# Register loads moved ahead of waits, and one root moved to ScalarE, in a two-layer graph network kernel

## The chip, the cores and the metric

One core of a Trainium2 chip. The metric is the device time of one execution in microseconds; the kernel before has a median of 3344.86 us over 3 runs (3327.63 to 3351.23). Its parts run on five engines with queues of their own: PE (matmul), DVE (vector), ACT (ScalarE), POOL (GpSimd) and SP, tied together by semaphores written out by hand.

## What is computed

A graph of 6250 nodes with 128 channels and 106250 edges, sorted by destination. First an attention layer, then an edge network with a sum over the incoming edges, each followed by a layer norm:

```python
hi, hj = x[src] @ w1, x[tgt] @ w2
logits = (leaky_relu(hi + hj, 0.3) * a).reshape(-1, 8, 16).sum(-1)
attn = exp(logits - segment_max) / segment_sum          # per destination
x = layernorm(x + segment_sum(hi * attn, tgt))
ef = (relu(edge_attr @ We1 + be1) @ We2 + be2) * sigmoid(ts @ Wt + bt)
msg = relu(concat([x[row], ef]) @ Wn1 + bn1) @ Wn2 + bn2
x = layernorm(x + segment_sum(msg, col) + x)
```

A layer norm divides by sqrt(variance + 1e-5).

## The kernel before

The edges are cut into NQ = 208 groups of 512 (QE). Destinations are sorted, so a group touches a window of at most 64 nodes (W) that begins at a base. The bases stand in `baseR`, and the columns of the table of hj that belong to a group in `tabR`, both in SBUF. Everything runs twice over the edges.

**Attention loop** (`run_steps`). A step handles GQ = 3 groups; there are NG = 70 steps, the last with one group. POOL (L707) gathers rows of `hi_rows` by index, 128 rows at a time, 4 gathers a group, into a ring of RG = 4 steps. On PE, `sums` adds to the transposed rows (L1826) the destination's part (L1831), ScalarE and DVE form the leaky value (L895, L1307), `quad_logits` (L1787) the logits. DVE scans for the maxima, makes one-hots of the window (L1389) and the messages (L1336), and `aggregate` on PE sums messages (L1854) and exponentials (L1858) over the window. DVE's `add` (L1310 to L1320) adds these sums at the window's base into `acc`. An `add` waits for `s_agg` (the sums) and `s_acc` (its own last add), then loads the base into a register, then adds. In `sums` PE waits for logits, gathered rows (`s_g`) and one-hots, and then loads the column. Batches of 3 node blocks (MB) are normalised in between. POOL waits for the messages of 3 steps ago before it refills a slot.

**Between the loops** the last steps A, Z and O (3, 3 and 1 groups) are written out, with adds of their own (L1442), then the last node blocks are normalised (L1404 to L1430) and written to `y_rows`. POOL waits for that write before it starts the second loop. In the drains PE runs some matmuls whose results nobody reads (`hold`, L1932, and L2055).

**Edge loop** (`run_edges`). One group a turn, in stages that lag each other: q is loaded and transposed, q-2 goes through the first layer (L2081, L1006), q-4 through the second (L2075) and the sigmoid (L994, L1629), q-6 is multiplied (L2069), added to the gathered row of `y_rows` (L1619) and passed through Relu (L999), q-8 is summed over the window (L2060) and added by DVE at its base (L1613). POOL (L741) gathers 4 times a group, up to 8 groups ahead of L1619. When a node block is complete (LOOPED = 45 of NB = 49 in the loop, one for every fourth group), PE multiplies its sum (L2096), DVE adds it to the row (L1578), takes moments (L1582, L1589), the reciprocal root, and scales (L1597); SP writes it out.

**The end.** After the last group DVE waits, PE multiplies the last 4 blocks (`rest`, L2101), and `finish`, `scale` and `normalise` do the same for all four at once, with tiles of 128x4. The reciprocal root of `inverse_root` is an iteration on DVE: variance + eps (L1167), two integer instructions (L1168, L1169) and three turns of three (L1171 to L1173), each waiting for the one before by semaphore `s_f["nr"]`, 11 counts (NEWTON) for each block.

ScalarE needs a function table in place: Exp in the attention loop, Sigmoid in the edge loop; Copy and Relu run with either.

Of the kernel before, what the change touches and what calls it, by code (L numbers as in the profile page):

```python
# [73 lines left out]
def build(nc, x, src, dst, attr, ew, w1, w2, a, We1, be1, We2, be2, Wt, bt, Wn1, bn1, Wn2, bn2,  # L74
          hi_d, y_d, x1_d, rel_d, scan_d, max_d, sum_d, agg_d, out):
    with ExitStack() as ctx:
# [703 lines left out]
        def _(act):  # L780
# [200 lines left out]
            with act.Else():  # L981
# [5 lines left out]
                def edge(q, r, k, m):  # L987
# [8 lines left out]
                    if z is not None:  # L996
                        act.wait_ge(s_b["zs"], z + 1)
                        need(act, s_b["agg"], z - 1)
                        act.activation(hS[i], zS[i], ACT.Relu).then_inc(s_b["h"], 1)  # L999
                        if not is_int(z) or z + RB < NQ:  # L1000

                            stage_b(z + RB, (r - L_Z) % RB)
                    if h is not None:
                        act.wait_ge(s_b["h1"], h + 1)
                        need(act, s_b["ef"], h - 1)
                        act.activation(r1S[i], h1P[i][:, :], ACT.Relu, bias=cols[:, 1:2]).then_inc(s_b["r1"], 1)  # L1006
                    if r % BQ == 0 and m is not None and (not is_int(m) or m < LOOPED):
                        act.wait_ge(s_b["acc"], (m + (LAG - 2)) * BQ)
                        need(act, s_f["o"], m)
                        act.activation(aF, accH[:, bass.ds(m * P, P)], ACT.Copy).then_inc(s_f["copy"], 1)  # L1010
                run_edges(act, edge)

        @block.vector
        def _(dve):
# [265 lines left out]
            with dve.Else():  # L1282
# [13 lines left out]
                def step(g, s, n, m):  # L1296
# [12 lines left out]
                    def add(j):  # L1309
                        if p is None or j >= quads(p):  # L1310
                            return
                        dve.wait_ge(s_agg, p * GQ + j + 1)
                        need(dve, s_acc, 2 * (p * GQ + j))
                        if is_int(p) and p == 0 and j == 0:
                            dve.wait_ge(s_zero, 18)
                        base = dve.value_load(baseR[0:1, bass.ds(p * GQ + j, 1)], min_val=0, max_val=NODES - 1)  # L1316
                        w_ = acc[:, 0, bass.ds(base, W)]
                        dve.tensor_tensor(w_, AG[j % 2][:, 0:W], w_, ALU.add).then_inc(s_acc, 1)  # L1318
                        w_ = accD[:, bass.ds(base, W)]
                        dve.tensor_tensor(w_, AG[j % 2][0:DC, W:2 * W], w_, ALU.add).then_inc(s_acc, 1)  # L1320
# [253 lines left out]
            with dve.Else():  # L1574
# [26 lines left out]
                def edge(q, r, k, m):  # L1601
# [3 lines left out]
                    if ends and r % BQ == 2:  # L1605
                        dve.wait_ge(s_x2, m + 1)
                        finish(m, 1, oP[:, 0:C], X1[:, bass.ds(m, 1), :].rearrange("p b c -> p (b c)"), xF, yF)
                    if g4 is not None:
                        dve.wait_ge(s_b["agg"], g4 + 1)
                        need(dve, s_b["acc"], g4)  # L1610
                        base = dve.value_load(baseR[0:1, bass.ds(g4, 1)], min_val=0, max_val=NODES - 1)
                        w_ = accH[:, bass.ds(base, W)]
                        dve.tensor_tensor(w_, sums_of(g4), w_, ALU.add).then_inc(s_b["acc"], 1)  # L1613
                    if z is not None:
# [32 lines left out]
                run_edges(dve, edge)  # L1647
                dve.wait_ge(s_x2, NB)
                finish(LOOPED, rest, ps[6][:, 0:rest * C], X1[:, LOOPED:NB, :].rearrange("p b c -> p (b c)"), xr, yr)
                scale(LOOPED, rest)  # L1650
                normalise(LOOPED, rest, xr, yr)


# [3 lines left out]
        def _(pe):  # L1657
# [125 lines left out]
            with pe.Else():  # L1783
# [17 lines left out]
                def step(g, s, n, m):  # L1801
# [7 lines left out]
                    def sums(j, of=None, os_=0, lj=0):  # L1809


                        if j >= nq:
                            logits(of, os_, lj)
                            return
                        lone = of is None or lj >= quads(of)
                        if not lone:
                            pe.wait_ge(s_lk, of * GQ + lj + 1)
                        pe.wait_ge(s_g[s][j], 64 * (n + 1) - 16 * (is_int(f) and f == NG - 1))
                        q = f * GQ + j
                        pe.wait_ge(s_ohT, q + 1)  # L1820
                        need(pe, s_lk, (f - 1) * GQ + j + 1)
                        col = pe.value_load(tabR[0:1, bass.ds(q, 1)], min_val=0, max_val=(2 * NB - 1) * 3 * C)

                        for i in range(4):
                            t = 4 * j + i
# [310 lines left out]
```

## Time and profile before

| what | value |
|---|---|
| median of 3 runs | 3344.86 us (3327.63 to 3351.23) |
| span of the profiled execution | 2205.4 us |
| busy: PE, DVE, ACT, POOL | 1817.9, 1325.7, 658.7, 1607.1 us |
| granted clock of PE, mean | 0.892 of full |
| chain that ended last, by engine | POOL 51%, issue 21%, PE 15%, DVE 5%, DMA 4% |
| gathers of the attention loop (L707) | 831, 804.1 us busy, 968 ns each |
| gathers of the edge loop (L741) | 831, 788.0 us busy, 948 ns each |
| adds in the attention loop's `add` (L1318), in the edge loop (L1613) | 201, 208, each 225 ns |

The span runs from the first to the last instruction of one execution under the profiler. The median of the runs is 1139.5 us longer; what lies in that difference the profile does not show. "issue" is time in which an engine waited for nothing that the profile shows. The chain is followed back from the last instruction to whatever released it, so it tells which engine's work set the end, where busy shares only tell who worked much.

### The profile page before, as it was taken

The numbers are of one execution on the slowest core, as the hardware profiler recorded it, in microseconds if no ns is written. First come the engines' busy times: TensorE is split into PE (matmuls) and PEld (weight loads), VectorE is DVE, ScalarE is ACT, GpSimd is POOL, SyncE is SP. The second block draws the span as 40 slices with busy tenths as digits, with TensorE's granted clock in tenths as the row PEclk, the third lists the DMA queues.
The fourth block names the chain that finished last, engine by engine and source line by source line (L and its number), as shares of the span: only waits on it lengthen the run. The fifth ranks groups of instructions, "written<-read, shape, count | busy, mean of one in ns | idle before, by whom it ended". The sixth has DMA issues, their size and how long they took to land.

```text
span 2205.4 us, 47181 instructions
## 1 busy us (share of the span) xinstructions
PE 1817.9 (82%) x12720; PEld 1413.0 (64%) x12721; DVE 1325.7 (60%) x3725; ACT 658.7 (30%) x1410; POOL 1607.1 (73%) x1701
## 2 busy tenths in 40 slices
PE   6778888888887788888879888888888888788887
PEld 6455666666665566666657667666766676667665
DVE  6454667565665666656645456666566666665665
ACT  6111112111121111111114344444444444444432
POOL 5777777777777777777517777777777777777775
PEclk9897879888799989888869999999999999899898
DMA  8722333333333333333245444444444444444441
GB/s 233 153 82 84 82 85 102 89 95 85 94 96 84 95 88 96 92 87 95 60 135 154 129 135 127 141 127 142 134 134 128 140 127 141 126 142 130 137 126 45
DMA packets 239385, 252.30 MB, mean 114 GB/s; under 512 B 141011, under 2 KB 187720, under 8 KB 239315
## 3 DMA queue, kind: packets, MB, share of 16 engines
q1 hardware_dynamic: 185036, 141.15, 21.5%
q0 software_dynamic: 54000, 110.28, 19.4%
q8 instruction: 30, 0.49, 0.1%
q14 instruction: 31, 0.25, 0.0%
q10 hardware_dynamic: 288, 0.13, 0.0%
HBM read 233.20 MB, written 13.22 MB: 112 GB/s over the span
## 4 chain that ended last, share of the span: by engine, by line
POOL 51%; issue 21%; PE 15%; DVE 5%; DMA 4%; DVEq 1%; POOLq 1%; ACT 1%; SPq 0%; ACTq 0%
POOL T L741 31%; POOL G L707 20%; PE ps L1854 3%; PE ps L1831 2%; DMA G<-hi_rows,idx 2%; PE ps L1826 2%; PE ps L1858 2%; PE ps L1787 1%; PE ps L2069 1%; DVEq L1316 1%; DVE msg L1336 1%; PE ps L2060 1%; DMA T<-y_rows,idx 1%; PE ps L2075 0%; ACT V L895 0%
## 5 line engine op out<-in xcount | busy, mean ns | idle before, releaser
L741 POOL DMA_INDIRECT T<-y_rows,idx x831 | 788.0, 948 | 310.2 <-issue 249.4
L707 POOL DMA_INDIRECT G<-hi_rows,idx x831 | 804.1, 968 | 263.3 <-issue 248.4
L2060 PE MATMUL ps<-G 128*128 128x64 f32 x1664 | 227.3, 283 | 117.5 <-DVE acc L1613 116.9
L999 ACT ACTIVATE G<-G 128x512 f32<-128x512 f32 x208 | 131.0, 630 | 582.4 <-DVE G L1619 582.4
L2060 PEld LDWEIGHTS ps<-G 128*128 128x128 f32 x1664 | 216.0, 203 | 129.4 <-issue 128.9
L1826 PE MATMUL ps<-ident,G 128*128 128x128 f32 x828 | 151.1, 312 | 161.7 <-issue 81.0
L1619 DVE TENSOR_TENSOR G<-ps,T 128x512 f32<-128x512 f32 x208 | 143.6, 690 | 225.9 <-DMA T<-y_rows,idx 217.4
L2069 PE MATMUL ps<-wN,G 128*128 128x128 f32 x1664 | 253.3, 300 | 28.5 <-DVE T L1578 28.4
L895 ACT ACTIVATE V<-ps 128x512 f32<-128x512 f32 x207 | 123.6, 597 | 464.3 <-PE ps L1831 463.8
L1854 PEld LDWEIGHTS ps<-oh,msg 128*128 128x128 f32 x1608 | 236.0, 222 | 33.2 <-issue 24.0
L1854 PE MATMUL ps<-oh,msg 128*128 128x64 f32 x1608 | 251.0, 307 | 1.4 <-DVE mX L1413 0.8
L1307 DVE TENSOR_TENSOR V<-ps,V 128x512 f32<-128x512 f32 x207 | 141.6, 684 | 177.5 <-ACT V L895 176.2
L2081 PEld LDWEIGHTS ps<-msg,wE 128*128 128x128 f32 x832 | 168.3, 203 | 124.1 <-issue 110.4
L2069 PEld LDWEIGHTS ps<-wN,G 128*128 128x128 f32 x1664 | 221.9, 207 | 31.2 <-DVE G L1629 31.0
L2075 PE MATMUL ps<-msg,wE 128*128 128x512 f32 x416 | 234.1, 647 | 0.0
L1826 PEld LDWEIGHTS ps<-ident,G 128*128 128x128 f32 x828 | 104.4, 157 | 201.4 <-issue 198.1
L2081 PE MATMUL ps<-msg,wE 128*128 128x256 f32 x832 | 223.6, 393 | 0.0
L1831 PE MATMUL ps<-ohT,T 128*128 128x512 bf16 x621 | 197.0, 432 | 0.0
L1318 DVE TENSOR_TENSOR acc<-ps,acc 128x64 f32 x201 | 45.2, 225 | 217.9 <-PE ps L1858 126.8
L994 ACT ACTIVATE G<-T,cols 128x512 f32<-128x512 f32 x208 | 166.9, 802 | 0.0
L1629 DVE SCALAR_TENSOR_TENSOR G<-ps,cols,G 128x512 f32<-128x512 f32 x208 | 154.8, 744 | 9.6 <-PE ps L2075 7.1
L1006 ACT ACTIVATE msg<-ps,cols 128x512 f32<-128x512 f32 x208 | 139.8, 672 | 38.1 <-PE ps L2081 37.8
(238 smaller groups left out, 2263.6 us busy)
## 6 DMA issues: line engine op xcount, KB each, us to landing
T<-in_edge_weight SPq DMA_DIRECT2D x103, 512.0 KB
Dbc<-block_destinations SPq DMA_DIRECT2D x69, 384.0 KB
T<-in_edge_attr SPq DMA_DIRECT2D x103, 256.0 KB
G<-hi_rows,idx POOLq DMA_INDIRECT x831
T<-y_rows,idx POOLq DMA_INDIRECT x831
link<-scan_destinations SPq DMA_DIRECT2D x280, 16.1 KB
hi_rows<-T SPq DMA_DIRECT2D x12, 256.0 KB, 4.4
mX<-in_x SPq DMA_DIRECT2D x15, 192.0 KB
```

Source lines behind the costliest of these rows:

```text
L707: pool.indirect_dma_start(out=G[:, s, t * C:(t + 1) * C], out_offset=None, in_=hi_d[:, :], in_offset=bass.IndirectOffsetOnAxis(ap=idx[:, s ...
L741: pool.indirect_dma_start(out=Yb[:, r, t * C:(t + 1) * C], out_offset=None, in_=y_d[:, :], in_offset=bass.IndirectOffsetOnAxis(ap=idx[:, r ...
L994: act.activation(twS[i], ewB[:, rr, :], ACT.Sigmoid, bias=cols[:, 4:5], scale=cols[:, 3:4]).then_inc(s_b["tw"], 1)
L1619: dve.tensor_tensor(zS[i], zP[i][:, :], Yb[:, rr, :], ALU.add).then_inc(s_b["zs"], 1)
L1629: dve.scalar_tensor_tensor(out=efS[i], in0=efP[i][:, :], scalar=cols[:, 2:3], in1=twS[i], op0=ALU.add, op1=ALU.mult).then_inc(s_b["efs"], 1)
L1826: pe.matmul(U[j][:, i * P:(i + 1) * P], G[:, s, t * C:(t + 1) * C], ident[:, :], is_transpose=True, start=(i == 0), stop=False, skip_group ...
L1831: ins = pe.matmul(U[j][:, :], flatT[:, bass.ds(col + part * C, C)], ohT[:, j, :], start=False, stop=(part == 2), skip_group_check=True)
L1854: pe.matmul(AG[j % 2][:, 0:W], msg[:, t * C:(t + 1) * C], oh[:, t * W:(t + 1) * W], start=(i == 0), stop=(i == 3))
L2060: ins = pe.matmul(sums_of(g4), hS[i][:, n * C:(n + 1) * C], ohB[i][:, n * W:(n + 1) * W], start=(n == 0), stop=(n == 3))
L2069: ins = pe.matmul(zP[i][:, n * C:(n + 1) * C], efS[i][:, n * P:(n + 1) * P], wN1[:, 1, :], start=True, stop=True)
L2075: pe.matmul(efP[i][:, :], wE2[:, :], r1S[i], start=True, stop=True).then_inc(s_b["ef"], 1)
L2081: ins = pe.matmul(out1[:, n], wE1[:, n, :], atS[i].rearrange("p (t e) -> p t e", t=2), start=True, stop=True)
```

## The change

Three register loads move in front of the waits that stood ahead of them: the base in the attention loop's `add`, the base in the edge loop's add, and the table column in `sums` on PE. The waits themselves stay. For the last four blocks, `scale` (moments, then `inverse_root`) is written out anew: moments, variance + eps on DVE, then a Sqrt on ScalarE, then a reciprocal on DVE. In turn 213 of the edge stages, behind the last Relu, ScalarE takes a Sqrt of one column (`pF`) into a part of `sd` that nothing reads. The 45 blocks inside the loop keep the iteration.

```diff
--- before.py
+++ after.py
@@ -1000,6 +1000,8 @@
                         if not is_int(z) or z + RB < NQ:
 
                             stage_b(z + RB, (r - L_Z) % RB)
+                    if is_int(q) and q == NQ + L_EF + 1:
+                        act.activation(sd[:, 1, 0:1], pF[:, :], ACT.Sqrt)
                     if h is not None:
                         act.wait_ge(s_b["h1"], h + 1)
                         need(act, s_b["ef"], h - 1)
@@ -1009,6 +1011,8 @@
                         need(act, s_f["o"], m)
                         act.activation(aF, accH[:, bass.ds(m * P, P)], ACT.Copy).then_inc(s_f["copy"], 1)
                 run_edges(act, edge)
+                act.wait_ge(s_f["nr"], NEWTON * LOOPED + 1)
+                act.activation(sd[:, 0, 0:rest], ve[:, 0, 0:rest], ACT.Sqrt).then_inc(s_f["nm"], 1)
 
 
 
@@ -1309,11 +1313,11 @@
                     def add(j):
                         if p is None or j >= quads(p):
                             return
+                        base = dve.value_load(baseR[0:1, bass.ds(p * GQ + j, 1)], min_val=0, max_val=NODES - 1)
                         dve.wait_ge(s_agg, p * GQ + j + 1)
                         need(dve, s_acc, 2 * (p * GQ + j))
                         if is_int(p) and p == 0 and j == 0:
                             dve.wait_ge(s_zero, 18)
-                        base = dve.value_load(baseR[0:1, bass.ds(p * GQ + j, 1)], min_val=0, max_val=NODES - 1)
                         w_ = acc[:, 0, bass.ds(base, W)]
                         dve.tensor_tensor(w_, AG[j % 2][:, 0:W], w_, ALU.add).then_inc(s_acc, 1)
                         w_ = accD[:, bass.ds(base, W)]
@@ -1606,9 +1610,9 @@
                         dve.wait_ge(s_x2, m + 1)
                         finish(m, 1, oP[:, 0:C], X1[:, bass.ds(m, 1), :].rearrange("p b c -> p (b c)"), xF, yF)
                     if g4 is not None:
+                        base = dve.value_load(baseR[0:1, bass.ds(g4, 1)], min_val=0, max_val=NODES - 1)
                         dve.wait_ge(s_b["agg"], g4 + 1)
                         need(dve, s_b["acc"], g4)
-                        base = dve.value_load(baseR[0:1, bass.ds(g4, 1)], min_val=0, max_val=NODES - 1)
                         w_ = accH[:, bass.ds(base, W)]
                         dve.tensor_tensor(w_, sums_of(g4), w_, ALU.add).then_inc(s_b["acc"], 1)
                     if z is not None:
@@ -1647,7 +1651,14 @@
                 run_edges(dve, edge)
                 dve.wait_ge(s_x2, NB)
                 finish(LOOPED, rest, ps[6][:, 0:rest * C], X1[:, LOOPED:NB, :].rearrange("p b c -> p (b c)"), xr, yr)
-                scale(LOOPED, rest)
+                dve.wait_ge(s_f["st"], LOOPED + 1)
+                for i in range(rest):
+                    ins = dve.bn_aggr(mv[:, 0, i, :], st[:, i, :])
+                ins.then_inc(s_f["mv"], 1)
+                dve.wait_ge(s_f["mv"], LOOPED + 1)
+                dve.tensor_scalar(ve[:, 0, 0:rest], mv[:, 0, 0:rest, 1], EPS, None, ALU.add).then_inc(s_f["nr"], 1)
+                dve.wait_ge(s_f["nm"], 1)
+                dve.reciprocal(rs[:, 0, 0:rest], sd[:, 0, 0:rest]).then_inc(s_f["rs"], 1)
                 normalise(LOOPED, rest, xr, yr)
 
 
@@ -1813,13 +1824,13 @@
                             logits(of, os_, lj)
                             return
                         lone = of is None or lj >= quads(of)
+                        q = f * GQ + j
+                        col = pe.value_load(tabR[0:1, bass.ds(q, 1)], min_val=0, max_val=(2 * NB - 1) * 3 * C)
                         if not lone:
                             pe.wait_ge(s_lk, of * GQ + lj + 1)
                         pe.wait_ge(s_g[s][j], 64 * (n + 1) - 16 * (is_int(f) and f == NG - 1))
-                        q = f * GQ + j
                         pe.wait_ge(s_ohT, q + 1)
                         need(pe, s_lk, (f - 1) * GQ + j + 1)
-                        col = pe.value_load(tabR[0:1, bass.ds(q, 1)], min_val=0, max_val=(2 * NB - 1) * 3 * C)
 
                         for i in range(4):
                             t = 4 * j + i
```

## Rows read from the trace of the kernel before

**Rows 1.** Busy time by stretch: length, PE, PEld, DVE, ACT, POOL, PE clock, DMA share, GB/s.

```profile
120.00:1088.00 968.00, 806.87 (x6641) 600.38 (x6641) 593.86 (x1575) 173.76 (x435) 736.08 (x762) 0.87 0.33 90
...
1145.00:2187.00 1042.00, 873.76 (x5070) 703.10 (x5070) 621.55 (x1855) 430.58 (x869) 788.01 (x831) 0.93 0.46 133
2187.00:2206.00 19.00, 7.33 (x38) 6.54 (x37) 6.72 (x30) 0.63 (x1) 0.01 (x1) 0.59 0.07 17
```

**Rows 2.** Waits of POOL: what waited, for what, us in total, times, longest.

```profile
POOL T L741 <- issue: 249.4, 818, 0.4
...
POOL T L741 <- DMA y_rows<-V: 57.1, 1, 57.1
...
POOL G L707 <- DVE msg L1336: 4.6, 15, 0.3
POOL T L741 <- ACT idx L983: 3.0, 10, 0.3
```

**Rows 3.** Chain that ended last, 2191 to 2196 us: start, us, what.

```profile
2192.02 0.30 DVEq L1611
...
2192.36 0.19 DVEq L1611
...
2192.58 0.02 DVEq L1611
...
2192.73 0.24 DVE acc L1613
...
2193.77 0.24 DVE acc L1613
...
2194.05 1.48 PE ps L2101 x8
```

**Rows 4.** Instructions in order of time, the end: start, us, engine, line, what.

```profile
2189.50 0.69 DVE L1619 TENSOR_TENSOR G<-ps,T 128x512 f32<-128x512 f32 x1 [1.21 <-DMA T<-y_rows,idx]
...
2190.22 0.63 ACT L999 ACTIVATE G<-G 128x512 f32<-128x512 f32 x1 [3.73 <-DVE G L1619]
2190.63 2.24 PE L2060 MATMUL ps<-G 128*128 128x64 f32 x16
...
2197.90 0.17 DVE L1167 TENSOR_SCALAR ve<-mv 128x4 f32<-128x4 f32 x1
...
2200.08 0.16 DVE L1173 SCALAR_TENSOR_TENSOR rs<-sd,rs 128x4 f32<-128x4 f32 x1
2200.28 1.11 DVE L1597 TENSOR_SCALAR T<-T,mv,rs 128x128 f32<-128x128 f32 x4
```

**Rows 5.** Instructions in order of time, the drain between the loops.

```profile
1098.33 0.61 PE L1858 MATMUL ps<-oh,EXs 128*9 128x64 f32 x8
...
1099.72 0.23 DVE L1318 TENSOR_TENSOR acc<-ps,acc 128x64 f32 x1 [0.82 <-PE ps L1858]
...
1099.93 1.56 PE L1932 MATMUL ps<-W,ident 128*128 128x256 f32 x6
...
1100.86 1.74 DVE L1449 TENSOR_TENSOR msg<-ps,G 128x1536 f32<-128x1536 f32 x1
...
1102.70 1.07 PE L1942 MATMUL ps<-oh,msg 128*128 128x64 f32 x8 [1.21 <-issue]
```

**Rows 6.** Groups of instructions by line, busy us, mean ns; then two instructions in time.

```profile
L983 ACT ACTIVATE idx<-IDX 128x4 int32 (+1 forms) x208 | 38.6, 189 | 0.0
...
L1407 DVE RECIPROCAL rd<-rd 128x24 f32<-128x24 f32 (+1 forms) x16 | 4.9, 306 | 0.5
...
1154.06 1.28 ACT L994 ACT_TABLE_LOAD   x1
1155.35 0.81 ACT L994 ACTIVATE G<-T,cols 128x512 f32<-128x512 f32 x1
```

**Rows 7.** Instructions in order of time: the same matmuls at two clock levels.

```profile
1078.20 1.97 PE L1854 MATMUL ps<-oh,msg 128*128 128x64 f32 x8
...
1094.45 1.10 PE L1854 MATMUL ps<-oh,msg 128*128 128x64 f32 x8
```

## The prediction

> **What bounds the kernel now.** I read the table of busy time by stretch first. The span has five parts: preparation up to about 31 us, the attention loop, a drain and refill around 1088 to 1145 us, the edge loop, and a drain of 19 us. In the two loops PE is busy 83% and 84% of the time and POOL 76%, so PE looks like the limit [rows 1]. The next view, what POOL waited for, turns this round: in the edge loop POOL issues 831 gathers of 0.948 us (the table of the profile) and before 818 of them it is idle for 249.4 us in all, 0.305 us each, with nothing to wait for. That is 1.25 us a gather, and 831 of them are 1041 us, the whole stretch from 1145.9 to 2187.0. The attention loop has the same 831 gathers. What POOL did wait for and another engine could have given earlier is small: 4.6 us for messages, in 15 pieces, and 3.0 us for staged indices, in 10; each piece is 0.3 us, the size of the plain issue gap, so even these are hardly waits [rows 2]. So in both loops POOL sets the pace: 4 gathers, 5.0 us, for each group of 512 edges. A faster DVE or PE there only waits longer for rows. The only large wait of POOL, 57.1 us, is the drain between the loops. Other engines set the time only there and behind POOL's last gather, which ends at 2187.01 us.
>
> **The loads ahead of the waits.** A register load is what the chain of waits shows as DVEq at L1611: pieces of 0.30, 0.19 and 0.02 us with gaps of 0.03, together 0.58 us (2192.02 to 2192.60), then 0.13 us of address arithmetic and dispatch before the add starts [rows 3]. The change moves the 0.58 us in front of the wait; the 0.13 us stay, since the window's address is computed behind it.
> In the loops this moves 201 adds in the attention loop's body (L1318), 208 in the edge loop (L1613) and the 207 loads of table columns on PE. I cost them at nothing: what hides them is POOL's 5.0 us a group, against which DVE is busy 621.55/208 = 3.0 us and PE 4.2 us [rows 1]. If that cover were gone they would be worth up to 0.58 us each, 237 us for the 409 adds. No engine gets a new wait: behind the moved load stands the same wait as before, and nothing else is queued between them. No DMA moves, and SP's and POOL's queues are untouched.
> In the last drain two adds lie on the path. PE's two last groups of sums run from 2190.63 for 2.24 us, to 2192.87; the second add starts at 2193.77, because it waited for the first add and then paid for its load [rows 3, 4]. With the loads ahead the first add can start at 2191.99 + 0.16 = 2192.15 and end at 2192.39; the second load runs under it, to about 2192.75; the second add starts 0.16 behind PE's end, at 2193.03. It is 0.74 us earlier. Bounds: nothing, if the sequencer can't read ahead of a running instruction, and 2 x 0.58 = 1.16 if both loads went out of the chain in full. The next thing late is PE's L2101, which needs only this add. I take 0.74, since the chain shows both loads exposed.
> In the middle drain one add lies on the path: PE's third group at L1858 ends at 1098.94, the add starts at 1099.72, then the one-hots (L1389), the message (L1449) to 1102.60, and PE, free since 1101.49, starts at 1102.70 [rows 5]. The add starts up to 0.58 us earlier and all that follows on DVE moves with it; PE stays free by then. I take 0.55. The adds behind it (L1442) are not changed. PE's column loads in this drain stand behind array work; the idle pieces before L1826 there are about 0.2 us, so three of them give at most 0.6 us more, taken as nothing. Bounds of this part: 0 to 1.2.
>
> **The root of the last four blocks.** Before, the 12 instructions of the iteration (L1167 to L1173) run from 2197.90 to 2200.24 and L1597 starts at 2200.28; the last block of work hangs on them alone [rows 4]. Of these the first stays, ending at 2198.07. The other eleven go, and in come one ScalarE root and one reciprocal over 128x4. The nearest rows: a ScalarE copy of 128x4 is 0.189 us; a reciprocal of 128x24 is 0.306 us, a plain DVE instruction of 128x4 0.16; a handover from DVE to ScalarE is 0.03 us (2190.19 to 2190.22) [rows 4, 6]. Cheapest: 0.03 + 0.19 + 0.03 + 0.16 + 0.03 = 0.44 us, L1597 at 2198.51, gain 1.77. Dearest, with handovers of 0.1 us, a root of 0.30 and a reciprocal of 0.306: 0.84 us, gain 1.37. I take 1.6, nearer the middle.
> The root needs another function table. The trace's load for the edge loop, at 1154.06, takes 1.28 us, and the next activation starts at 1155.35 [rows 6]. The early root (on pF, into a part of sd that nothing reads) stands behind ScalarE's last Relu, which ends at 2190.85 [rows 4]; a load there ends at about 2192.2, 5.9 us before the real root can start. ScalarE has nothing else to do, so its price is nothing; without that cover it would be 1.28 us.
> The Trainium skill (ScalarE: Activation LUTs, What ACT_TABLE_LOAD costs) gives 1.283 us for the load and about 1.38 us more of drain, 2.66 us for a switch; the load agrees with the trace, but no drain of that size stands behind it in the rows. By the page the table would be there at about 2193.5, still early, and the sum would be the same.
>
> **The sum.** 0.74 + 0.55 + 1.6 = 2.9 us. The profiled execution becomes 2205.4 - 2.9 = 2202.5 us. The runs' median of 3344.86 us is 1139.5 us above that span; nothing in the trace says what these are, and the change has nothing in it that would move time outside the first and last instruction, so I carry them over unchanged: 3344.86 - 2.9 = 3342.0 us. That is 0.09%, while the three runs shown lie between 17.2 below and 6.4 above their median. A measurement of this kernel can tell about 1% (33 us) from no change.
>
> **Rivals.**
> *Less than that.* The sequencer does not read ahead, or its hidden loads are replaced by the handovers: 0 + 0 + 1.37 us and less, about 3344. For it: the second add needs its load under a running add, which no row of before shows. Against it: PE's and DVE's queues elsewhere start 0.03 us behind a release. 0.13.
> *The table comes late.* The early root is placed by hand, but the load is placed by the compiler, at the real root: 1.28 us in the chain, gain 2.9 - 1.28 = 1.6 us, about 3343. For it: no row shows a load placed by an early use. Against: a root cannot run before its table. 0.05. The Trainium skill (ScalarE activation tables: per-element evaluation and per-set limits, Table sets in the compiler and the runtime) has the loads placed block by block for the longest run of functions; with its pair of 1.28 and 1.38 us in the chain the gain would be 0.2 us.
> *Faster by over 1%.* The timed executions, 1139.5 us longer than the span, may be paced by the chain of DVE and PE instead of by POOL; then the exposed loads count in the loops, up to 409 x 0.58 = 237 us, about 3105. For it: the unexplained difference. Against it: the same program is in the trace, with POOL's cadence of 1.25 us throughout and waits for others of under 10 us. It decides only if a group took over 5.0 us on the chain. 0.06.
> *Slower by over 1%.* PE's clock. In the attention loop the granted clock is 0.87 of full, so about 0.26 of the time lies at the lower level; the same eight matmuls of L1854 take 1.10 us at one level and 1.97 at the other, 1.79 times as long [rows 1, 7]. PE's work is then 806.87 x (0.74 + 0.26 / 1.79) = 714 us at the full clock, and 0.16 of it runs at the lower one. Other idle times of PE, from loads and adds that come earlier, could shift that share. PE alone would need 968 + 33 us from a share of (1001 / 714 - 1) / 0.79 = 0.51; that is the point where it costs 1%, about 3378. Against it: PE's work and its 5.0 us a group are unchanged, and idle pieces under 0.6 us move. 0.03.
>
> **How the numbers follow.** The forecast has 0.73, the two small rivals 0.18; all three lie within 1%, so same is 0.91, faster 0.06 and slower 0.03. The bounds of the costs alone give gains from 1.4 (or 0.1 with the late table) to 1.77 + 1.16 + 1.2 = 4.1 us, 3340.7 to 3344.8. Wider than that is the scatter of the runs, 17.2 us to one side; around 3342.0 it gives 3325 to 3359. That is the range; it leaves out the two large rivals, 0.09 together.
>
> **What would show it.** In the changed kernel's trace: POOL's 831 gathers still at 1.25 us, its idle time before them still about 249 us in the edge loop; the wait of 57.1 us for the written rows down to about 56.5; the two last adds at L1613's line 0.6 us closer to PE's sums with no register load between them; one more table load between 2190 and 2193; the scale step of the last four blocks about 0.5 us long instead of 2.2. It would be wrong if POOL's cadence moved at all, if a table load appeared inside the edge loop, or if the time fell by tens of microseconds with the span unchanged.

## The result, and the profile after

The kernel after the change takes 3310.93 us (3302.07 to 3329.34, 13 runs); the kernel before, on the same chip, 3344.86 us (3327.63 to 3364.26, 13 runs). The ratio is 0.9899, with a 95% interval of 0.9878 to 0.9921: 34 us faster, where 2.9 were forecast. The time lies outside the range of 3325 to 3359.

The first lines of the page of the kernel after:

```profile
span 3307.2 us, 47103 instructions
...
PE 2016.5 (61%) x12650; PEld 1517.1 (46%) x12721; DVE 1325.7 (40%) x3715; ACT 663.0 (20%) x1413; POOL 1590.4 (48%) x1701
```

The span is 3307.2 us, only 3.7 less than the median of the runs, and 1.8 less than the time of that same execution (3309.01 us). In the trace of before that was shown, the span was 2205.4 us against a median of 3344.86. The engines are busy for about as long as they were there, PE for longer (2016.5 against 1817.9 us); what has grown is the idle time between. Busy time by stretch (length, PE, PEld, DVE, ACT, POOL, PE's clock, DMA share, GB/s), the attention loop and the edge loop of the kernel after, from the first to the last gather of each:

```profile
31.00:1804.00 1773.00, 929.28 (x7020) 657.08 (x7087) 644.48 (x1670) 199.59 (x485) 787.00 (x831) 0.69 0.21 57
...
1862.00:3270.00 1408.00, 994.11 (x4925) 781.06 (x4926) 603.56 (x1798) 423.68 (x853) 787.95 (x831) 0.82 0.36 98
```

The same 831 gathers, as long as ever in sum, now lie in 1773 and 1408 us instead of 1057 and 1041. A group of 512 edges takes 1773 / 208 = 8.5 us and 1408 / 208 = 6.8 us, where POOL needs 5.0. What the engines waited for, in the kernel after (us in total, times, longest):

```profile
DVE acc L1322 <- remote: 778.2, 101, 13.5
...
POOL G L707 <- DVE msg L1340: 691.3, 60, 46.1
...
POOL T L741 <- ACT idx L983: 344.9, 80, 7.7
```

POOL waited 691.3 us for messages and 344.9 us for staged indices; in the trace of before these were 4.6 and 3.0 us [rows 2]. DVE waited 778.2 us for sums in 101 pieces, and the profile names no releaser ("remote"), since PE's matmuls had by their records long ended. POOL does not set the pace here. So the two traces first had to be brought onto one footing.

### The profile page after: what moved, and what is told of

Its sections match the earlier page's. It is cut to its first block, busy times and chain, and to the rows that moved or that the text cites. A ratio compares the mean times of both kernels' runs of the same rounds, so it can differ in the third digit from the quotient of the medians.

```text
span 3307.2 us, 47103 instructions
## 1 busy us (share of the span) xinstructions
PE 2016.5 (61%) x12650; PEld 1517.1 (46%) x12721; DVE 1325.7 (40%) x3715; ACT 663.0 (20%) x1413; POOL 1590.4 (48%) x1701
## 4 chain that ended last, share of the span: by engine, by line
PE 35%; another core or an unknown queue 29%; issue 16%; DVE 10%; DVEq 4%; ACT 1%; SPq 1%; DMA 1%; ACTq 0%
PE ps L2080 6%; PE ps L1842 5%; PE ps L1837 4%; PE ps L2086 4%; PE ps L2071 4%; PE ps L2092 3%; PE ps L1798 3%; PE ps L1865 2%; PE ps L1869 1%; DVEq L1613 1%; DVE G L1633 1%; DVEq L1316 1%; PE ps L2101 1%; DVE R L1369 1%
## 5 line engine op out<-in xcount | busy, mean ns | idle before, releaser
L707 POOL DMA_INDIRECT G<-hi_rows,idx x831 | 787.3, 947 | 996.0 <-DVE msg L1340 691.3
L741 POOL DMA_INDIRECT T<-y_rows,idx x831 | 787.9, 948 | 677.5 <-ACT idx L983 344.9
L1837 PE MATMUL ps<-ident,G 128*128 128x128 f32 x828 | 193.8, 375 | 667.8 <-issue 621.2
L1837 PEld LDWEIGHTS ps<-ident,G 128*128 128x128 f32 x828 | 135.3, 193 | 729.6 <-issue 727.7
L2071 PE MATMUL ps<-G 128*128 128x64 f32 x1664 | 260.4, 309 | 202.9 <-DVE acc L1617 102.9
L1322 DVE TENSOR_TENSOR acc<-ps,acc 128x64 f32 x201 | 45.2, 225 | 836.7 <-remote 778.2
L2071 PEld LDWEIGHTS ps<-G 128*128 128x128 f32 x1664 | 243.7, 225 | 225.5 <-issue 199.7
L2080 PE MATMUL ps<-wN,G 128*128 128x128 f32 x1664 | 296.5, 334 | 40.2 <-DVE T L1582 34.6
L2080 PEld LDWEIGHTS ps<-wN,G 128*128 128x128 f32 x1664 | 261.7, 239 | 44.3 <-DVE G L1633 32.4
L2086 PE MATMUL ps<-msg,wE 128*128 128x512 f32 x416 | 271.3, 738 | 3.0 <-issue 2.7
L1865 PE MATMUL ps<-oh,msg 128*128 128x64 f32 x1608 | 216.2, 277 | 1.1 <-issue 0.8
L1865 PEld LDWEIGHTS ps<-oh,msg 128*128 128x128 f32 x1608 | 202.1, 193 | 27.9 <-issue 16.1
L2101 PE MATMUL ps<-ident,T 128*128 128x128 f32 x416 | 87.3, 294 | 175.1 <-DVE msg L1638 86.0
```

The lines of the kernel that those rows point to most:

```text
L707: pool.indirect_dma_start(out=G[:, s, t * C:(t + 1) * C], out_offset=None, in_=hi_d[:, :], in_offset=bass.IndirectOffsetOnAxis(ap=idx[:, s ...
L741: pool.indirect_dma_start(out=Yb[:, r, t * C:(t + 1) * C], out_offset=None, in_=y_d[:, :], in_offset=bass.IndirectOffsetOnAxis(ap=idx[:, r ...
L1837: pe.matmul(U[j][:, i * P:(i + 1) * P], G[:, s, t * C:(t + 1) * C], ident[:, :], is_transpose=True, start=(i == 0), stop=False, skip_group ...
L1865: pe.matmul(AG[j % 2][:, 0:W], msg[:, t * C:(t + 1) * C], oh[:, t * W:(t + 1) * W], start=(i == 0), stop=(i == 3))
L2071: ins = pe.matmul(sums_of(g4), hS[i][:, n * C:(n + 1) * C], ohB[i][:, n * W:(n + 1) * W], start=(n == 0), stop=(n == 3))
L2080: ins = pe.matmul(zP[i][:, n * C:(n + 1) * C], efS[i][:, n * P:(n + 1) * P], wN1[:, 1, :], start=True, stop=True)
```

## The experiments

**The kernel before, unchanged, and its parts, on one chip.** Four kernels: before again; the three loads alone; the root alone; PE's column load alone. Each part has the lines of the diff that stand ahead of the prediction, and the fourth is this:

```diff
                         lone = of is None or lj >= quads(of)
+                        q = f * GQ + j
+                        col = pe.value_load(tabR[0:1, bass.ds(q, 1)], min_val=0, max_val=(2 * NB - 1) * 3 * C)
                         if not lone:
                             pe.wait_ge(s_lk, of * GQ + lj + 1)
...
-                        col = pe.value_load(tabR[0:1, bass.ds(q, 1)], min_val=0, max_val=(2 * NB - 1) * 3 * C)
```

> The kernel before, unchanged, for a profile of an execution like those that were timed. The profile shown ahead of the prediction has a span of 2205 us where the timed runs take 3345. Theory: the timed executions have long pauses in the chain of PE and DVE that the shown execution had not; then this span is about 3340 us, POOL waits hundreds of us for messages and indices, and sums of PE reach DVE microseconds late. Rival: the 1139 us lie outside the span; then the span is about 2205 us and the time about 3345.

> Only the three register loads stand ahead of their waits; the root of the last four blocks stays the iteration on DVE. Theory (the chain of PE and DVE paces the timed runs, and exposed loads count in it): all of the gain, ratio about 0.990 (33 us less). Rival (the gain comes from the end or from another source): ratio within 0.2% of 1.

> Only the root of the last four blocks goes to ScalarE; the loads stay behind their waits. Theory: 1.6 us less, ratio 0.9995, not to be told from 1. Rival (the end costs far more in the timed runs than in the profile): ratio about 0.990.

> Only PE's load of the table column moves ahead of its waits, 207 times in the attention loop; DVE's bases stay behind theirs. If the load on PE is exposed each time at about 0.6 us, up to 69 steps x 0.6 = 41 us or, at two of three hidden, less: ratio 0.990 to 0.996. Rival (the gain is DVE's bases): ratio within 0.2% of 1.

The kernel before took 3333.25 us here (median of 23 runs). Unchanged, it gave 3330.94 us with a span of 3328.9: there is no difference of 1139 us between span and time, the span itself is long. loads_only took 3307.27 us (6 runs), ratio 0.9915 [0.9884, 0.9946], 26 us faster. root_only was 1.0009 [0.9979, 1.0039] and pe_load_only 0.999 [0.9964, 1.0017]. So the gain comes with the loads. PE's load alone gives nothing that can be told from zero (its interval reaches 12 us), and the root's 1.7 us are below what can be told.

The waits of before, unchanged, on this chip:

```profile
POOL G L707 <- DVE msg L1336: 690.8, 60, 48.5
...
DVE acc L1318 <- remote: 645.8, 83, 12.9
```

They are much as in the kernel after, so they are not the change's work: the two traces compared until now come from different surroundings. One such wait, in order of time (start, us, engine, line, what; in brackets the idle time before), before unchanged:

```profile
1002.45 0.23 DVE L1318 TENSOR_TENSOR acc<-ps,acc 128x64 f32 x1
...
1002.91 0.62 PE L1858 MATMUL ps<-oh,EXs 128*9 128x64 f32 x8
...
1004.96 0.78 PE L1858 MATMUL ps<-oh,EXs 128*9 128x64 f32 x8
...
1013.53 0.22 DVE L1318 TENSOR_TENSOR acc<-ps,acc 128x64 f32 x1 [9.63 <-remote]
...
1015.59 1.11 PE L1826 MATMUL ps<-ident,G 128*128 128x128 f32 x4 [9.84 <-issue]
...
1018.36 0.22 DVE L1318 TENSOR_TENSOR acc<-ps,acc 128x64 f32 x1 [3.76 <-remote]
```

The three adds belong to the three groups of one step. PE's sums of the second group end, by the records, at 1003.53, and the add that waits for them starts at 1013.53; those of the third end at 1005.74, and their add starts at 1018.36. PE has no record for 9.84 us and starts again only 2 us behind the second add. The chain of waits over the same place (start, us, what) tells when DVE was let go:

```profile
1003.90 8.72 another core or an unknown queue
...
1012.64 0.04 DVEq L71
...
1012.82 0.30 DVEq L1316
...
1013.16 0.19 DVEq L1316
...
1013.53 0.09 DVE acc L1318
...
1013.81 0.47 DVE R L1376
...
1014.31 0.06 DVE XM L1380
```

DVE was let go at 1012.62, 9.1 us behind the recorded end of the second group's sums. Behind that stands the load (0.30 and 0.19 us), then the add, a scan and the subtraction XM, on which the exponentials and PE's next work hang. From release to add it takes 0.91 us. And the clock there, from busy time by stretch (columns as above, the clock third from the end), before unchanged:

```profile
1005.00:1006.00 1.00, 0.74 (x9) 0.43 (x8) 0.00 (x0) 0.00 (x0) 0.70 (x1) 1.00 0.26 66
1006.00:1008.00 2.00, 0.00 (x0) 0.00 (x0) 0.00 (x0) 0.00 (x0) 1.69 (x2) 0.78 0.24 64
1008.00:1010.00 2.00, 0.00 (x0) 0.00 (x0) 0.00 (x0) 0.00 (x0) 1.39 (x3) 0.50 0.14 35
```

PE works at the full clock until 1005.7, the clock falls to half between 1006 and 1008, and the sums reach DVE at 1012.6. The semaphore of the third group's sums rose at 1017.44, 11.7 us behind its recorded end and even behind the start of PE's next record. So "no record" does not show that PE had nothing to do.

Counted over the whole loop, PE's semaphore rose over 1.5 us behind the recorded end of the sums in 136 of the 201 groups: in 65 of 67 second groups, 65 of 67 third ones and 6 of 67 first ones. The median over all 201 is 5.3 us. In the trace shown before the prediction it was 1 of 201. Counted over all matmuls that raise a semaphore (delays of 1.5 to 15 us, overlapping ones taken together), that trace has 29 late stretches, 133 us in all, and this one 176, 1669 us in all. The trace lacks some semaphore events (200 of 208 of these sums are in it), so a single delay is rough.

The kernel after, at such a place, in its chain of waits:

```profile
407.55 0.30 DVEq L1316
...
408.12 0.02 DVEq L1316
408.14 9.55 another core or an unknown queue
...
417.90 0.09 DVE acc L1322
```

Its load is done at 408.14, ahead of the wait. DVE is let go at 417.69 and the add starts at 417.90, 0.21 us later instead of 0.91. That is 0.70 us saved at a place where PE's next step waits for DVE's XM.

How much of the loop's adds lose such time is in their groups (count, busy, mean ns, idle time before them, by releaser), first of before unchanged, then of loads_only, on the same chip:

```profile
L1318 DVE TENSOR_TENSOR acc<-ps,acc 128x64 f32 x201 | 45.3, 225 | 894.0 <-remote 645.8 <-issue 191.8 <-PE ps L1858 56.2
```

```profile
L1318 DVE TENSOR_TENSOR acc<-ps,acc 128x64 f32 x201 | 45.2, 225 | 837.4 <-remote 766.3 <-issue 47.2 <-PE ps L1858 23.7
```

The idle time ahead of the 201 adds fell by 56.6 us, 0.28 us an add, and "issue", where the loads stand, from 191.8 to 47.2; the wait named "remote" grew in its place, from 645.8 to 766.3, since DVE now begins it earlier. In the edge loop the same move did much less: "issue" ahead of the 208 adds of L1613 is 94.5 us in before and 88.4 in loads_only. There the profile has a wait for late sums ahead of only 46 of the 208 adds in before; where the wait is already over, the load costs DVE its time on either side of it. PE's own waits for these adds, ahead of L2060, fell from 112.7 to 77.9 us. From the first to the last gather the edge loop took 1415.5 us in before and 1412.7 in loads_only, one execution each.

**The base loads one by one, and the reverse.** attention_bases moves only the load of L1316, edge_bases only that of L1611, each by the lines of the change. bases_twice is before with each base loaded twice behind its wait:

```diff
                         base = dve.value_load(baseR[0:1, bass.ds(p * GQ + j, 1)], min_val=0, max_val=NODES - 1)
+                        base = dve.value_load(baseR[0:1, bass.ds(p * GQ + j, 1)], min_val=0, max_val=NODES - 1)
...
                         base = dve.value_load(baseR[0:1, bass.ds(g4, 1)], min_val=0, max_val=NODES - 1)
+                        base = dve.value_load(baseR[0:1, bass.ds(g4, 1)], min_val=0, max_val=NODES - 1)
```

add_later is the kernel after, with the attention loop's second add behind the last scan and XM, which PE waits for, instead of ahead of them:

```diff
                     nxt(2)
-                    add(1)
...
                         dve.tensor_tensor(XM[0:BR, :], logit, R4[0:BR, :], ALU.subtract).then_inc(s_xm, 1)
+                    add(1)
```

> Only DVE's load of the base in the attention loop moves ahead of its waits (three adds a step, L1311 to L1316). Theory: in a step DVE waits about 10 us for sums of PE, and behind that wait stand the load, the add, a scan and the row maxima that PE waits for; two loads of 0.58 us in 68 steps, or one where the second overlaps: 28 to 50 us less, ratio 0.985 to 0.992, most of what all loads gave. Rival (the edge loop holds the gain): ratio within 0.2% of 1.

> Only DVE's load of the base in the edge loop moves ahead of its waits. Theory: DVE has other work between its waits there and POOL waits less, so at most 10 us less, ratio 0.997 to 1.000. Rival (the gain is in the edge loop): ratio about 0.991.

> The kernel before with each base of DVE loaded twice behind its waits, in both loops; the second register is what the add uses. Theory: exposed load time counts on the chain, so the loss is as large as the gain of the loads ahead: 28 to 50 us more, ratio 1.008 to 1.015. Rival (the gain comes from another order of waits and instructions, not from the load's time): ratio within 0.3% of 1.

> The changed kernel, and in the attention loop DVE's second add of a step stands behind the last scan and the subtraction of the maxima instead of ahead of them. Theory: PE's next step waits for these maxima, and the second add, 0.5 us and more with its wait, stood in front of them in each of 68 steps: 25 to 45 us less than the changed kernel, ratio to the kernel before 0.977 to 0.982. Rival (what paces the step is a fixed pause of PE that begins by time and not by the chain): ratio as the changed kernel, 0.990.

On this chip the kernel before took 2200.73 us (30 runs), a third less than in the two sets of runs above. attention_bases was 1.002 [1.0005, 1.0035], edge_bases 0.9995 [0.9979, 1.0012], add_later 0.9995 [0.998, 1.001]; bases_twice 1.0055 [1.0034, 1.0076], 10.5 us. None of the first three gained. Nor did bases_twice lose the 28 to 50 us that were expected. The expectations rested on the long level, and these runs were not at it; so they say nothing on where the 34 us come from. They say that at this level the loads are hidden, as the prediction had it, with one reservation: 409 second loads of at most 0.58 us cost 10.5 us, 0.026 us each, so the cover is not quite whole. The drains, where the prediction has three adds on the path, will have part of it.

**The kernel after at the shorter level, and three of the edits again.**

> The changed kernel once more, beside the kernel before on the same chip. Two levels of time have been seen for the kernel before: 3333 to 3345 us in three sets of runs and 2201 us in one, each the same through its set. Theory: which level it is belongs to the chip, and the gain exists only at the slow level, where late sums of PE pace the loops: ratio 0.990 if the kernel before takes about 3340, and 0.998 to 1.000 (2.9 us less by the prediction's sum, perhaps) if it takes about 2200. Rival (the gain is there at either level): ratio 0.990 in both.

> Only the bases of the attention loop ahead of their waits, as before. At the slow level, theory: ratio 0.985 to 0.993, most of the gain. At the fast level: 1.000 to 1.003, as measured there. Rival (at the slow level the gain lies in the edge loop): ratio within 0.3% of 1 there.

> Only the bases of the edge loop ahead of their waits. At the slow level, theory: ratio 0.996 to 1.000; rival: about 0.991. At the fast level: 0.999 to 1.000, as measured there.

> The changed kernel with DVE's second add of a step behind the row maxima. At the slow level, theory: 25 to 45 us less than the changed kernel, ratio 0.977 to 0.983 to the kernel before. Rival (PE's late stretches begin by time, not by the chain): as the changed kernel, 0.990. At the fast level: 0.999 to 1.000, as measured there.

This chip was at the same level: before 2201.16 us (35 runs). after_again took 2198.8, ratio 0.999 [0.9977, 1.0004], 2.4 us. The others: 1.002 [1.0004, 1.0036], 0.999 [0.9972, 1.0007] and 0.9992 [0.9978, 1.0007]. Waits and attention loop of the kernel after at this level:

```profile
POOL T L741 <- issue: 249.2, 817, 0.4
```

```profile
31.00:1088.00 1057.00, 854.37 (x7098) 652.26 (x7166) 650.59 (x1684) 203.04 (x491) 804.78 (x828) 0.87 0.35 95
```

POOL's idle time before the gathers of the edge loop is 249.2 us in 817 pieces, to set beside [rows 2], and PE's clock in the attention loop 0.87 as in [rows 1]. The adds in their groups, of the kernel after at this level:

```profile
L1322 DVE TENSOR_TENSOR acc<-ps,acc 128x64 f32 x201 | 45.2, 225 | 185.7 <-PE ps L1869 179.3 <-issue 5.9
```

The kernel before had 217.9 us there, 90.8 of them "issue". So the loads left the place behind the wait here too, 32 us of DVE's idle time with them, and the end moved by 2.4 us, because POOL waits for none of it. The one oddity is attention_bases at +0.2% on two chips (3.3 and 3.5 us), with intervals that exclude no change, while the kernel that holds the same edit and the others of the change loses nothing. Its cause is open.

**Making the loop of sums long on purpose.** If lateness of PE is what exposes the load, more work on PE should do so too. The message matmuls of the second group of each step (L1854) run 11 times instead of once, each time anew from zero:

```diff
-                        for i in range(4):
-                            t = 4 * j + i
+                        for i in range(4 * (11 if j == 1 else 1)):
+                            t = 4 * j + i % 4
                             pe.matmul(AG[j % 2][:, 0:W], msg[:, t * C:(t + 1) * C], oh[:, t * W:(t + 1) * W],
-                                      start=(i == 0), stop=(i == 3))
+                                      start=(i % 4 == 0), stop=(i % 4 == 3))
```

long_before has this in before, long_bases with the load of attention_bases too, long_later in add_later. attention_bases_3 is attention_bases, without the long work.

> The kernel before with work of PE made longer in each step of the attention loop: the eight matmuls that sum the messages of the second group (L1854) run 11 times over instead of once, the same result each time, 10 x 0.97 us = 9.7 us more a step. It stands for the late sums of the slow level, on any chip. Theory (chips at the fast level only lack PE's late stretches): at the fast level the step no longer fits the 15 us of POOL's gathers, POOL waits hundreds of us for messages, and the time rises from 2201 by 68 x 7 to 10 us, to about 2700 to 2900. Rival (POOL still hides it): under 2300.

> The same long PE work, and DVE's bases of the attention loop ahead of their waits, nothing else of the change. Theory: where PE's sums come last, the loads count on any chip: 28 to 80 us less than the kernel with long PE work alone. Rival (the gain belongs to something else in the slow level): the same time as that kernel, within 7 us.

> The same long PE work in the changed kernel with DVE's second add behind the row maxima. Theory: 20 to 40 us less than long PE work with the bases ahead alone. Rival: the same as that one within 7 us.

> Only the bases of the attention loop ahead of their waits, PE's work as before. If the kernel before takes about 3340 us on this chip, theory: ratio 0.985 to 0.993; rival (gain in the edge loop): within 0.3% of 1. If it takes about 2200: 1.002, as measured twice.

This chip was at the long level: before 3256.57 us (17 runs). attention_bases_3 took 3243.81 us (12 runs), ratio 0.9949 [0.9921, 0.9977]: the attention loop's base load alone is worth 13 us here (17 by the ratio, 7 to 26 by its interval), where it was worth nothing or less on two others. long_before took 3967.49, long_bases 3962.43 and long_later 3909.86 us (6 runs each), ratios 1.2164 [1.2116, 1.2212], 1.2148 [1.21, 1.2197] and 1.1975 [1.1929, 1.2022]. The long work cost 711 us, 10.5 a step. The load alone gained 5 us with it, less than the intervals can tell from nothing; the expectation of tens fell. long_bases in order of time, at one such place:

```profile
1221.12 0.23 DVE L1318 TENSOR_TENSOR acc<-ps,acc 128x64 f32 x1 [22.38 <-PE ps L1858]
...
1221.27 1.95 PE L1854 MATMUL ps<-oh,msg 128*128 128x64 f32 x8
...
1224.10 1.12 PE L1826 MATMUL ps<-ident,G 128*128 128x128 f32 x4
```

Behind the late sums PE has a group of its own to do (1221.27 to 1224.17), so it does not wait for DVE, and an add earlier by 0.6 us frees nobody. The idle time ahead of the transposing matmuls (L1826), which begin each step and each group, says the same of the whole loop (count, busy, mean ns, idle time before them, by releaser), first in before unchanged, then in long_bases:

```profile
L1826 PE MATMUL ps<-ident,G 128*128 128x128 f32 x828 | 193.8, 378 | 674.3 <-issue 445.8 <-DVE XM L1380 226.4 <-DVE V L1307 1.7
```

```profile
L1826 PE MATMUL ps<-ident,G 128*128 128x128 f32 x828 | 175.6, 350 | 52.2 <-issue 48.6 <-DVE V L1307 1.7 <-DVE XM L1380 1.5
```

In before unchanged PE has a gap in its records ahead of the first L1826 in 66 of 68 steps, 9.8 us in the median, and then starts 1 us behind the end of DVE's XM; in long_bases it has one in 13 of 68. So the load counts where PE's next step waits for DVE, and not merely where the sums come after long work of PE. The long work is also no copy of the long level's lateness: in long_bases no group's semaphore rose over 1.5 us behind its record. That PE is free to start earlier in those gaps is argued from its records; the semaphores that rise behind them leave it open, and could be why attention_bases_3 gained 13 us and not 48. long_later is another 53 us faster than long_bases; in the profiles 41 us of it lie in the attention loop. It differs by the place of the second add, and by the root, the edge load and PE's load too, so the place of the add is likely, but was not isolated.

**Two of the edits once more.**

> Only the bases of the edge loop ahead of their waits. The attention loop's alone gave 0.9949 where the kernel before took 3257 us, all loads together 0.9915 where it took 3333. If the kernel before takes over 3200 us on this chip, theory (both loops share the gain): ratio 0.994 to 0.998. Rival (the rest of the gain is noise of the chips): within 0.2% of 1. At the fast level: 0.999, as measured twice.

> The changed kernel with DVE's second add behind the row maxima. With long PE work this step gave 53 us over the bases ahead alone. At the slow level, theory: 20 to 45 us less than the changed kernel, ratio 0.977 to 0.985. Rival (PE's late stretches begin by time and eat what the chain gives): as the changed kernel, 0.990. At the fast level: 0.999, as measured twice.

Before 2200.41 us (23 runs); edge_bases_3 0.9998 [0.9984, 1.0013], add_later_3 0.9986 [0.9973, 0.9999]. The chip was again at the shorter level, so what the edge loop's load and the add's place are worth at the long level stays open. add_later is at no point shown to beat the kernel after.

## Why the prediction was wrong

**The step that failed.** It is the sentence "nothing in the trace says what these are, and the change has nothing in it that would move time outside the first and last instruction, so I carry them over unchanged", said of the 1139.5 us between span and median. They lie inside the span. The same kernel takes 3345, 3333 and 3257 us in three sets of runs and 2200.7, 2201.2 and 2200.4 us in three others, each set on one chip and steady, with spans of 3328.9 and 2205.4 us. The trace shown came from an execution at one level, the timed runs from the other. With it fell the cost that was set for the loads: "I cost them at nothing: what hides them is POOL's 5.0 us a group". A gap of 34% between span and median was the signal; the bottleneck was then argued from a trace that was not of the timed execution.

**POOL sets the pace.** True in the shown trace (1.25 us a gather) and in after_again. In the timed executions it is false: 8.5 and 6.8 us a group. The point that the prediction set for its rival, "only if a group took over 5.0 us on the chain", was passed in both loops.

**The cover of the loads.** In the timed executions it is not there. The cost of a load was right in kind and size (0.58 us): 0.91 us from release to add falls to 0.21, 0.70 less. The rival "Faster by over 1%" had the mechanism, and got 0.06. Its price was an upper bound of 237 us, every load in full; measured were 26 us for all loads and 34 for the change. Where PE's next step waits for DVE, about once a step, 68 x 0.70 = 48 us could be gained in the attention loop, an estimate from the 0.70 us above; attention_bases_3 gives 7 to 26 us for that loop. How the rest divides between the edge loop and scatter is not settled: 0.9915 and 0.9949 were measured on different chips, and the edge loop's part was timed only at the shorter level.

**PE's column loads, nothing.** The number is right, 0.999 [0.9964, 1.0017] at the long level, but not for the reason given. The edit moves the load ahead of the waits inside `sums`. At the start of a step another wait, for XM, stands ahead of the first `sums`, in both kernels:

```python
                    if f is not None:

                        need(pe, s_xm, f - 1)
                    sums(0, b, bs, 2)
```

The chain of pe_load_only at such a place (start, us, what):

```profile
921.53 0.30 DVE XM L1380
921.83 1.15 issue
922.98 1.08 PE ps L1826 x4
```

The 1.15 us behind XM hold the moved load. In the median of 68 steps PE starts 1.12 us behind XM with the load moved, and 0.99 in before unchanged. So the first load of a step was never taken off PE's path. One ahead of the wait for `s_xm` was not run.

**The end.** Right, and of the size forecast. The last instructions of the kernel after, in order of time:

```profile
3295.66 1.90 PE L2071 MATMUL ps<-G 128*128 128x64 f32 x16
3295.77 0.63 ACT L999 ACTIVATE G<-G 128x512 f32<-128x512 f32 x1 [1.72 <-DVE G L1623]
3296.42 1.28 ACT L1004 ACT_TABLE_LOAD   x1
...
3297.69 0.23 DVE L1617 TENSOR_TENSOR acc<-ps,acc 128x64 f32 x1 [0.68 <-PE ps L2071]
...
3301.40 0.17 DVE L1659 TENSOR_SCALAR ve<-mv 128x4 f32<-128x4 f32 x1
3301.60 0.21 ACT L1015 ACTIVATE sd<-ve 128x4 f32<-128x4 f32 x1 [3.69 <-DVE ve L1659]
3301.84 0.18 DVE L1661 RECIPROCAL rs<-sd 128x4 f32<-128x4 f32 x1 [0.27 <-ACT sd L1015]
3302.06 1.12 DVE L1601 TENSOR_SCALAR T<-T,mv,rs 128x128 f32<-128x128 f32 x4
```

From variance to scale it takes 3302.06 - 3301.40 = 0.66 us, where it took 2.38 [rows 4]: 1.72 gained, 1.6 forecast. The second add starts 0.13 us behind PE's end (3297.56), instead of 0.90 [rows 3, 4]; 0.16 was forecast. The table load stands where the early root is, 0.02 us behind the last Relu, and is over 3.9 us before the real root, so the rival of the late table is out.

**The sum.** At the level of the shown trace, 2.9 us forecast and 2.4 measured (-0.9 to 5.1 by the interval, so the time alone does not tell it from nothing). Its terms can be read in the trace of after_again. The middle drain there, in order of time:

```profile
1098.15 0.22 DVE L1322 TENSOR_TENSOR acc<-ps,acc 128x64 f32 x1 [0.18 <-PE ps L1869]
...
1101.13 1.07 PE L1953 MATMUL ps<-oh,msg 128*128 128x64 f32 x8 [0.58 <-issue]
```

PE's third group ends at 1098.01, so it is 3.12 us to the next sums, where it was 3.76 [rows 5]: 0.64 us gained, 0.55 forecast. In the last drain the second add starts 0.14 us behind PE's end instead of 0.90: 0.76 gained, 0.74 forecast. From variance to scale it takes 0.65 us: 1.73 gained, 1.6 forecast. Together 3.1 us. The wait for the written rows, which was to fall from 57.1 to 56.5 us, is 48.4 there, but 49.4 in edge_bases, which leaves that drain as it was; it scatters by more than the term. The sum held there; it was applied to runs at the other level.

## What to carry to other kernels

Compare the profile's span with the timed runs before reading a single wait; here an execution's own span is some 2 us below its time. If they differ by much more than the runs scatter, the profiled execution was not like the timed ones, and every "hidden behind" drawn from it needs its own check against a slower clock or a later engine. Work that is independent of a wait (a register load, an address) belongs ahead of it even where it looks covered: the change cost nothing at one level, and its loads were worth 0.8% at the other, though the attention loop's alone was 0.2% slower in two sets of runs. Whether such a load pays depends on who waits for the engine when its own wait ends: with PE at work on its next group it gained nothing, with PE waiting for XM it gained. And find the wait that ends last before moving a load: PE's went ahead of the waits beside it and stayed behind the one that counted.

## What the runs showed of the hardware that was not expected

One program has two levels, 2200 to 2201 us and 3257 to 3345, with mean granted clocks of TensorE of 0.892 and 0.754 in the two traces of before. A set of runs was at one level throughout. No chip is known to have been used in two sets, so whether the level belongs to the chip or to the occasion was not tested. The lower clock does not explain the longer time by itself: at 1008 in the rows above PE has nothing recorded to do, at whatever clock, and its results are still under way. The long work shows such a stretch from inside, with matmuls recorded in it. long_before in order of time, one second group with its 88 recorded matmuls:

```profile
1232.29 5.12 PE L1854 MATMUL ps<-oh,msg 128*128 128x64 f32 x44
...
1237.68 0.65 PE L1854 MATMUL ps<-oh,msg 128*128 128x64 f32 x4 [0.26 <-issue]
...
1240.54 1.10 PE L1854 MATMUL ps<-oh,msg 128*128 128x64 f32 x4 [0.45 <-issue]
...
1247.58 5.18 PE L1854 MATMUL ps<-oh,msg 128*128 128x64 f32 x24 [1.83 <-issue]
```

and two stretches of it:

```profile
1232.00:1237.00 5.00, 5.00 (x51) 4.80 (x51) 1.49 (x5) 0.00 (x0) 3.78 (x5) 1.00 0.20 52
...
1240.00:1245.00 5.00, 2.59 (x10) 2.16 (x10) 0.00 (x0) 0.00 (x0) 3.78 (x5) 0.50 0.21 52
```

At the full clock 44 matmuls take 5.12 us, 0.116 us each. Then 20 take 9.9 us (1237.68 to 1247.58), 0.50 us each with gaps in which nothing is recorded, and the last 24 take 5.18, 0.216 each. The granted clock reads 0.88 in the mean from 1237 to 1240, and from there on 0.50, which is 1.2 of 2.4 GHz. At that level eight of these matmuls take 1.97 us, 0.246 each [rows 7]; but the 11 from 1240.54 to 1247.58 take 7.04 us, 0.64 each. So for some 10 us PE went at half the speed that its recorded clock would give, or less. In both places this follows a stretch of dense work at the full clock and comes with its fall; that is a pattern in the rows, not a cause shown. The Trainium skill (TensorE: Matmul & The Clock Gate, Seeing it yourself) warns that clock records in a trace can be unreliable and that TensorE has been seen held at a quarter of its clock for over 50 us. 0.50 us against 0.116 is near such a quarter, but the stretches here are some 10 us long, and no run here could show the true clock. Why some sets of runs show this and others hardly do was not found.

An early activation places its table load by hand: 1.28 us at 3296.42, and the next activation of ScalarE starts 0.01 us behind its end. The further drain of about 1.38 us that the Trainium skill (ScalarE: Activation LUTs, What ACT_TABLE_LOAD costs) gives is not in the rows, on either side of the load.
